# Causal attention inside a fused layer: fewer score maxima ahead of attention, folds between them, and maxima that go straight into the query operand

## The reference, cut to what matters

```python
def _attn(x, ln_w, ln_b, conv_w, attn_w, proj_w, n_head):
    h = _layernorm(x, ln_w, ln_b)
    ...  # causal convolution of 3 taps per channel
    q, k, v = jnp.split(h @ attn_w, 3, axis=-1)
    ...  # heads of D = 8, rotary embedding of q and k
    scores = jnp.einsum('bqhd,bkhd->bhqk', q, k) / jnp.sqrt(jnp.float32(D))
    scores = jnp.where(jnp.tril(jnp.ones((T, T), dtype=bool)), scores, jnp.float32(-1e+30))
    p = jax.nn.softmax(scores, axis=-1)
    y = jnp.einsum('bhqk,bkhd->bqhd', p, v).reshape(B, T, C)
    return y @ proj_w
```

## Time and profile before

| | |
|---|---|
| median of 3 runs | 385.88 us (384.13 to 386.39) |
| the profiled execution's own time | 381.65 us |
| its span, first to last instruction | 379.8 us |
| mean granted clock of TensorE | 0.953 |
| PE busy | 330.6 us (87%) |
| DVE busy | 244.9 us (64%) |
| ACT busy | 210.6 us (55%) |
| POOL busy | 99.3 us (26%) |

### The profile page before, as it was taken

The page is one execution under the profiler, slowest core; times in us unless marked ns, Lnnn a source line. Parts: engine busy times, 40 slices in busy tenths (PEclk is TensorE's granted clock), DMA queues, the critical chain, the costliest instruction groups (busy, mean ns, idle before and its releaser), DMA issues.

```text
span 379.8 us, 6492 instructions
## 1 busy us (share of the span) xinstructions
PE 330.6 (87%) x2287; PEld 224.6 (59%) x2287; DVE 244.9 (64%) x606; ACT 210.6 (55%) x619; POOL 99.3 (26%) x110
## 2 busy tenths in 40 slices
PE   2768999998999699999988995997889999999756
PEld 1236888664656345545534663565568788887645
DVE  5785865785898757733623651236977976886746
ACT  1377795273234345565675532233676766776984
POOL 3425572110600000000140121041267454445300
PEclk9997999999999669999999998799999999999986
DMA  7660000076963000009001002020001000000001
GB/s 227 193 196 2 2 0 2 10 251 173 301 181 94 10 0 2 2 16 325 6 28 50 0 14 63 2 76 1 24 27 29 0 3 0 3 0 3 0 2 55
DMA packets 21506, 22.53 MB, mean 59 GB/s; under 512 B 3517, under 2 KB 18269, under 8 KB 21469
## 3 DMA queue, kind: packets, MB, share of 16 engines
q1 hardware_dynamic: 19666, 20.02, 17.4%
q0 software_dynamic: 512, 1.05, 0.9%
q10 hardware_dynamic: 1296, 1.05, 0.9%
HBM read 14.32 MB, written 7.70 MB: 58 GB/s over the span
## 4 chain that ended last, share of the span: by engine, by line
PE 53%; DVE 24%; issue 6%; DMA 6%; ACT 5%; POOL 4%; POOLq 0%; ACTq 0%; DVEq 0%
PE PS L1198 45%; PE PS L1241 5%; DVE mB L774 5%; ACT big L1027 3%; DMA big<-scr_x 2%; DVE big L633 2%; POOL scr_x L525 2%; DVE XN L578 2%; DVE stats L567 1%; DMA X<-in_x 1%; DVE big L595 1%; DMA scr_x<-XN,pos 1%; DVE mraw L587 1%; DVE big L971 1%; PE PS L1208 1%
## 5 line engine op out<-in xcount | busy, mean ns | idle before, releaser
L1198 PE MATMUL PS<-big 128*128 128x128 f32 (+10 forms) x592 | 103.8, 324 | 12.5 <-DVE mB L774 4.9
L1198 PEld LDWEIGHTS PS<-big 128*128 128x128 f32 (+3 forms) x592 | 61.3, 155 | 50.3 <-issue 18.0
L1001 ACT ACTIVATE big<-PS 128x1280 f32<-128x1280 f32 (+2 forms) x44 | 41.0, 934 | 48.2 <-PE PS L1241 31.2
L482 POOL TENSOR_TENSOR big<-big,urec 128x1024 f32<-128x1024 f32 x24 | 45.6, 1900 | 65.8 <-DVE urec L626 44.6
L1027 ACT ACTIVATE big<-big 128x154 f32<-128x154 f32 x192 | 60.4, 319 | 4.1 <-DVE big L633 2.9
L1135 ACT ACTIVATE big<-PS 128x1024 f32<-128x1024 f32 (+3 forms) x64 | 42.6, 703 | 33.2 <-PE PS L1198 33.1
L774 DVE TENSOR_REDUCE mB<-PS 128x2 f32<-128x256 f32 (+5 forms) x86 | 51.0, 648 | 13.8 <-PE PS L1198 13.1
L1198 PE MATMUL PS<-cstb 128*128 128x128 bf16 x256 | 50.9, 228 | 0.0
L470 POOL TENSOR_TENSOR rstd<-ve,minus_half 128x4 f32<-128x4 f32 (+2 forms) x13 | 13.1, 1011 | 137.1 <-DVE ve L573 137.1
L1198 PE MATMUL PS<-kkC,XT 128*128 128x462 f32 (+1 forms) x96 | 36.2, 512 | 2.6 <-DVE big L633 2.6
L1027 ACT ACTIVATION_READ_ACCUMULATOR big<-big 128x1 f32 x192 | 36.3, 189 | 0.0
(11 more groups left out here) (174 smaller groups left out, 439.6 us busy)
## 6 DMA issues: line engine op xcount, KB each, us to landing
scr_qk<-big SPq DMA_DIRECT2D x12, 384.0 KB, 3.7
big<-scr_qk SPq DMA_DIRECT2D x16, 288.0 KB
big<-in_wv SPq DMA_DIRECT2D x1, 2048.0 KB, 9.5
scr_x<-zrow SPq DMA_DIRECT2D x2, 448.0 KB, 6.4
big<-scr_x SPq DMA_DIRECT2D x2, 448.0 KB, 4.3
scr_y<-big SPq DMA_DIRECT2D x2, 448.0 KB, 3.0
X<-in_x ACTq DMA_DIRECT2D x2, 256.0 KB, 3.7
big<-in_A_WoT ACTq DMA_DIRECT2D x1, 512.0 KB, 4.6
```

The source lines that it names most:

```text
L482: pool.tensor_tensor(pn[:, 0:GH * P].rearrange("p (h k) -> p h k", h=GH), Pt[u % 3][:, :, 0:KM], r.to_broadcast([P, GH, KM]), ALU.mult).th ...
L1001: return act.activation(dst, src, ACT.Copy, scale=scale)
L1198: return pe.matmul(o, lhsT, rhs, start=start, stop=stop)
```

## The change

- `PREC`: the vw/vr jobs of groups 2 and 3 (eight) come last; 42 jobs stand ahead of them (`F_VALUES`), and 46 ahead of those of group 3 (`F_BETWEEN`).
- Between the maxima of sequence 0 there is a fold after each odd m from 3, up to job 45. The other four follow after maxima 33 to 36, with their banks exchanged; job 47 needs the bank of the transposed maxima and waits for the first of their parts.
- `M_MERGE` is 38 (was 42) and `M_TURN` 33 (was 34): six maxima of sequence 1 ahead of attention, transposition after 32; `S_MAX` becomes 13 (was 11).
- Each of the three parts has its own semaphore step (`m_part`) and its own DMA from `nm3` to one row of `qs`; the scratch `scr_m` is gone.
- Attention's first pair waits for reduce 36, its second for 37 (both waited for 41).
- ScalarE lays out `vaug` from job 42 on, between four of the last copies.

```diff
+        F_VALUES = 42
+        F_BETWEEN = 46
...
-                if c >= 2 and c % 2 == 0:
+                if c in (2, 4):
                     for b in range(B):
                         yield "vw", (c // 2 - 1, b), 1
                         yield "vr", (c // 2 - 1, b), 1
+            for g in (2, 3):
+                for b in range(B):
+                    yield "vw", (g, b), 1
+                    yield "vr", (g, b), 1
...
         def fold_bank(n):
-            return n % 3 if n < F_LATE else 6 + n % 2
+            if n < F_LATE:
+                return n % 3
+            return 6 + n % 2 if n < F_BETWEEN else 7 - n % 2
...
-        M_TURN = 32 + 2
-        M_MERGE = 32+10
+        M_TURN = 32 + 1
+        M_MERGE = 32 + 6
         S_MAX = (64 - M_MERGE) // 2
...
             for b in range(B):
-                sp.wait_ge(m_split, b + 1)
-                sp.dma_start(scr_m[b].rearrange("a (n q) -> n a q", q=P), nm3[:, b]).then_inc(m_written[b], 16)
-                sp.wait_ge(m_written[b], 16)
                 sp.wait_ge(*((s1_mm, 2 * (64 - M_MERGE)) if b else (s_mm, 32)))
-                sp.dma_start(qs[b][SPLIT:SHIFT, :, :],
-                             scr_m[b].rearrange("a (h t) -> a h t", h=HB)).then_inc(m_ready[b], 16)
+                for a in range(3):
+                    sp.wait_ge(m_part[b], a + 1)
+                    sp.dma_start(qs[b][SPLIT + a:SPLIT + a + 1].rearrange("r h (t q) -> r (h t) q", q=P),
+                                 nm3[:, b, a]).then_inc(m_ready[b], 16)
...
-                own(dve.tensor_copy(nm3[:, b, 0], nmf[:, 0]))
-                own.wait()
+                dve.tensor_copy(nm3[:, b, 0], nmf[:, 0]).then_inc(m_part[b], 1)
+                dve.wait_ge(m_part[b], 1)
                 own(dve.tensor_tensor(nmf[:, 1], nmf[:, 0], nm3[:, b, 0], ALU.subtract))
                 own.wait()
-                own(dve.tensor_copy(nm3[:, b, 1], nmf[:, 1]))
-                own.wait()
-                dve.tensor_tensor(nm3[:, b, 2], nmf[:, 1], nm3[:, b, 1], ALU.subtract).then_inc(m_split, 1)
+                dve.tensor_copy(nm3[:, b, 1], nmf[:, 1]).then_inc(m_part[b], 1)
+                dve.wait_ge(m_part[b], 2)
+                dve.tensor_tensor(nm3[:, b, 2], nmf[:, 1], nm3[:, b, 1], ALU.subtract).then_inc(m_part[b], 1)
...
-            copy_C(F_LN, len(PREC))
-            def stack_values():
-                act.wait_ge(preC_act, N_PREC)
-                for b in range(B):
...
-            stack_values()
+            copy_C(F_LN, F_VALUES)
+            act.wait_ge(preC_act, sum(j[2] for j in PREC[:F_VALUES]))
+            for b in range(B):
...
+                copy_C(F_VALUES + 2 * b, F_VALUES + 2 * b + 1)
...
+                copy_C(F_VALUES + 2 * b + 1, F_VALUES + 2 * b + 2)
+            copy_C(F_VALUES + 2 * B, len(PREC))
...
+                    elif n == F_BETWEEN + 1:
+                        pe.wait_ge(m_part[0], 1)
...
                 if m == M_MERGE:
-                    pe.wait_ge(m_split, 1)
+                    pe.wait_ge(m_part[0], 1)
+                    pe.wait_ge(preC_act, N_PREC)
...
             for m in range(32):
                 scores_for_maximum(m)
-                if m >= 2 and m % 2 == 0 and late < len(PREC):
+                if m >= 3 and m % 2 == 1 and late < F_BETWEEN:
                     fold_C(late, late + 1)
                     late += 1
-            fold_C(late, len(PREC))
-            for m in range(32, M_MERGE):
+            for m in range(32, M_TURN):
                 scores_for_maximum(m)
-                if m == M_TURN - 1:
-                    pe.wait_ge(preC_act, N_PREC)
-                    turn_maxima(0)
+            pe.wait_ge(preC_act, sum(j[2] for j in PREC[:F_BETWEEN]))
+            turn_maxima(0)
+            for m in range(M_TURN, M_MERGE):
+                scores_for_maximum(m)
+                if late < len(PREC):
+                    fold_C(late, late + 1)
+                    late += 1
...
-                    pe.wait_ge(m_ready[b], 16)
+                    pe.wait_ge(m_ready[b], 16 * 3)
...
-                        pe.wait_ge(s_max, M_MERGE)
+                        pe.wait_ge(s_max, M_MERGE - 1 + pair)
```

More of the change, by code:

```diff
@@ L238, in program @@
         scr_y = [nc.dram_tensor(f"scr_y{b}", (SLOTS * P, D), F32, kind="Internal").ap() for b in range(B)]
-        scr_m = nc.dram_tensor("scr_m", (B, 3, HB * QT * P), BF16, kind="Internal").ap()
         F_UNIT = (3, 6, 9)
@@ L305, in program @@
         s1_mm, s1_max = sem("s1_mm"), sem("s1_max")
-        m_turned, m_split = sem("m_turned"), sem("m_split")
-        m_written = [sem(f"m_written{b}") for b in range(B)]
+        m_turned = sem("m_turned")
+        m_part = [sem(f"m_part{b}") for b in range(B)]
         m_ready = [sem(f"m_ready{b}") for b in range(B)]
@@ L1097, in _ @@
             ln_out("b", HT[:, :, 2:T + 2], *ln1, seqs=(1,))
-            copy_C(F_LN, len(PREC))
-            def stack_values():
-                act.wait_ge(preC_act, N_PREC)
-                for b in range(B):
-                    v = vaug[:, b].rearrange("p t h m -> p (t h) m")
-                    copy(v[:, :, 0:HDB], XN[:, QT * b:QT * b + QT, :].rearrange("p t (h d) -> p (t h) d", h=HB)).then_inc(v_ready, 1)
-                    copy(v[:, :, HDB:HDB + 1], ones[:, 0:QT * HB].unsqueeze(2)).then_inc(v_ready, 1)
-                    copy(v[:, :, HDB + 1:32], ones[:, 0:32 - HDB - 1].unsqueeze(1).to_broadcast([P, QT * HB, 32 - HDB - 1]),
-                         0.0).then_inc(v_ready, 1)
-            stack_values()
+            copy_C(F_LN, F_VALUES)
+            act.wait_ge(preC_act, sum(j[2] for j in PREC[:F_VALUES]))
+            for b in range(B):
+                v = vaug[:, b].rearrange("p t h m -> p (t h) m")
+                copy(v[:, :, 0:HDB], XN[:, QT * b:QT * b + QT, :].rearrange("p t (h d) -> p (t h) d", h=HB)).then_inc(v_ready, 1)
+                copy(v[:, :, HDB:HDB + 1], ones[:, 0:QT * HB].unsqueeze(2)).then_inc(v_ready, 1)
+                copy_C(F_VALUES + 2 * b, F_VALUES + 2 * b + 1)
+                copy(v[:, :, HDB + 1:32], ones[:, 0:32 - HDB - 1].unsqueeze(1).to_broadcast([P, QT * HB, 32 - HDB - 1]),
+                     0.0).then_inc(v_ready, 1)
+                copy_C(F_VALUES + 2 * b + 1, F_VALUES + 2 * b + 2)
+            copy_C(F_VALUES + 2 * B, len(PREC))
             act.wait_ge(scr_written[B - 1], 16 * 6)
@@ L1404, in turn_maxima @@
                 if b:
-                    pe.wait_ge(m_split, b)
+                    pe.wait_ge(m_part[0], 1)
                 pe.transpose(PS[0:HB * QT, 6, 0:P], mB[:, b].rearrange("p h t -> p (h t)"), ident).then_inc(m_turned, 1)
@@ L1466, in turn_outputs @@
                         pe.wait_ge(yg_ready, 4 * b + 4)
-                        pe.wait_ge(m_split, B)
+                        pe.wait_ge(m_part[B - 1], 1)
                         if b:
```

## The result

| | before | changed | ratio, 95% interval |
|---|---|---|---|
| median, first measurement | 385.71 us | 375.81 us (373.66 to 379.54) | 0.9741 [0.9691, 0.9791] |
| median, second measurement | 384.45 us | 377.28 us | 0.9783 [0.9733, 0.9833] |
| profiled execution, first measurement | 381.65 us, span 379.8 | 373.66 us, span 371.8 | |

The changed kernel is faster by 2.2 to 2.6%. Medians are of all executions of a kernel and ratios leave out its slow ones (over 1.5% above its fastest; one of four and one of six here), so the second ratio says -8.3 us where its medians say -7.2. The forecast was 378.9, in a range of 375.5 to 383.0; the first median lies 0.3 us above the range's lower end. The first question is where the 8.0 us between the two spans lie, since a trace is one execution.

A forecast was written before the change was run, and what follows sets the result against it. Three limits: a TensorE-VectorE loop, a hole, then TensorE alone, half of that at half clock. Terms -5.7 - 3.3 + 1.35 + 0.7 = -6.95 us took the median from 385.88 to 378.9, range 375.5 to 383.0.

The forecast's parts named there:

- end of the last reduce of sequence 0: Loop of sequence 0's maxima: moved folds spare three head pairs 0.35 us each, 1.05; taken as 1.0, bounds 0.3 to 1.1.
- from there to attention: Last reduce of sequence 0 to attention's start: 5.0 us instead of 9.74; with the earlier reduce, attention starts 5.7 sooner.
- attention, steps 0 to 4: Start of attention: the clock holds, so steps 0 to 3 take 9.76 instead of 13.02 us, -3.3.
- four tiles more: Attention steps 11 and 12: four more score tiles of sequence 1 cost +1.35 us (1.2 to 1.6).
- stand at step 16: Attention step 16: TensorE waits for sequence 1's maxima, transposed after step 13, not 11; +0.7 us (0 to 1.5).
- so VectorE's own sum binds: Loop of sequence 0's maxima: with folds moved, the two-engine loop falls under VectorE's 3.06 us a head pair.
- busy until T0+4.9: After sequence 0's last reduce (T0): transposition, five score tiles and four folds keep TensorE busy for 4.9 us.
- landed at T0+4.0, hidden by 0.9: Third part of sequence 0's maxima, issued 1.9 us after the last reduce (T0), lands at 4.0, 0.9 before attention needs it.
- B: Rival: the clock falls all the same in the hole before attention, the 3.3 us are gone, -3.65, 382.2 us; chance 0.13.
- C: Rival: direct DMAs are slow, 1.7 us a part, stands before attention and at step 16; +3.75, 389.6 us; chance 0.09.
- D: Rival: later stages' stands meet the clock otherwise and give back 3 us; -4, 381.9 us; chance 0.15.
- The row against the rule: Maxima transfers: a trace row's 197 GB/s was trusted over the port rule's some 27 GB/s, which would give -6.1 in all.

The follow-up runs named there:

- the even folds: Changed kernel with the 14 folds between sequence 0's maxima back behind even m (2 to 28); ratio 0.9853 to the kernel before.
- early-transposition kernel: Changed kernel with sequence 1's maxima transposed ahead of step 12's output matmuls, not behind; 374.83 against 383.17 us, again 375.03 against the changed kernel's 377.28.
- the fold ahead: Changed kernel with fold 46 moved ahead of the transposition of sequence 0's maxima, the other three behind maxima 34 to 36; 376.18 against 383.17 us.
- both moves: Changed kernel with fold 46 ahead of sequence 0's transposition and sequence 1's transposition ahead of step 12's output matmuls; 375.18 against 383.17 us.
- the load held: Changed kernel with the 2 MB expert weight load waiting on SyncE until step 16's first pair is scored; 377.83 against 384.45 us.

## Why the prediction came out as it did

By its own terms, with the changed kernel's first profile beside them:

| term | forecast | measured |
|---|---|---|
| end of the last reduce of sequence 0 | -1.05 | -2.12 (25.64 to 23.52 from the first reduce) |
| from there to attention | 5.0 for 9.74: -4.7 | 6.47: -3.27 |
| attention, steps 0 to 4 | -3.3 | -3.87 |
| four tiles more | +1.35 | +1.44 (19.26 - 1.16 - 16.66) |
| stand at step 16 | +0.7 | +1.16 |
| sum | -6.95 | -6.65 |

The mechanism was right. That the sum is this close is luck: the loop gave 1.1 us more than forecast and the way to attention 1.4 less.

**The loop.** The step "so VectorE's own sum binds" was right, its size was not. I took 3.06 for that sum because the timeline prints 16 reduces as one block of 12.22 us. A block without idle time in it doesn't say that the engine sets its pace: the even folds give 3.06 with both engines in the chain, VectorE was busy for 12.08 us of that block, and the new kernel gives 2.94. That is 8 x 0.12 = 1.0 us, nearly the whole error of this term (1.07).

**From there to attention.** Two things failed here, and either is enough. In the first profile it was the clock: "busy until T0+4.9" held for 1.00, and with some 3 us at half TensorE's own work fills 6.34 us. The third part wasn't last there. At full clock the share was sized rightly: in the early-transposition kernel TensorE works from 119.43 to 124.37, 4.94 us. There "landed at T0+4.0, hidden by 0.9" failed. Each issue takes 0.46 to 0.60 us and not 0.3 to 0.4, three in a row take 1.81, and in five of the profiles (the fold ahead, the early transposition, both moves, the load held, the changed kernel again) the slowest landing of sequence 0 took 3.3 to 3.8 us from its issue. In these five the clock was at 1.00 in this stretch, and attention starts 5.6 to 6.0 us behind the transposition, once that part is there. In all five, and in the even folds with 2.8, a 16 KB instruction packet started before the parts had all moved, and four packets of a part moved only at its end, as shown above. In the other five profiles with direct parts, and for sequence 1 in all eleven, no such packet ran beside them, and no landing took more than 2.3. What makes that packet come when it does, no experiment took apart.

**The clock.** In attention it held, as forecast, and by the first profile that is the largest term: 3.9 us. The forecast had it at 1.00 from 95 to 160. Around the transposition it was at 0.50 for 3.4 us in the changed kernel, in its forms with the scratch back and with ten maxima, and in the second profile of the early transposition, and for 6.8 us in the even folds. All five had a stand of 1.56 or 1.60 us ahead of the transposition, not the 1.1 of the forecast. So had the three profiles in which it held; behind 0.42 and 0.43 it held twice. Between two profiles of one kernel a fall of 3.4 us made 0.3 us (the changed kernel) and 0.6 (the early transposition), since where the clock holds the late third part costs something too; the fall of 6.8 cost 1.9.

A low clock in steps 0 to 4 costs 3 to 4.6: they took 12.2 to 13.8 us in seven kernels, and 9.15 or 9.16 in the others. The stand right ahead of step 0 (1.27 to 3.49 us in the seven) isn't the cause in all of them. In the kernel before, with direct DMAs alone and with six maxima alone the clock was already down when that stand began; it had fallen at the end of the one of 1.63 us or just behind it. With direct DMAs and six maxima it fell 0.2 us after that stand began. It fell behind that stand in three: ten maxima (1.64), the fold ahead (1.97) and both moves (1.52). Behind 1.43, 1.06, 1.03 and 0.71 us it held, and behind the 2.10 us of the earlier trace rows too, so length alone doesn't decide. What the change did is to leave no stand of over 1.1 us between the transposition and step 0.

**Four tiles and step 16.** Both were sized from the right rows. The stand is 0.5 longer than forecast, from the same three issues of 0.58. It is gone when the second transposition comes 1.6 us earlier (13.23 us behind step 8's first matmul, not 14.83).

**The rest of the distance.** The median is 3.1 us below the forecast, while the region alone gained 0.3 less than it. The changed kernel's runs lie from 373.66 to 382.34, and its two profiles differ by 6.5 us outside the region (371.8 - 68.17 and 377.9 - 67.81), with identical code. By the ratios the gain is 10.0 us (8.1 to 11.9) and 8.3 (6.4 to 10.3). The second holds the 6.95 and the 7.0 of its region, the first holds neither. Some 1.3 to 3.4 us of gain outside the region stay open: the kernel before has one profile, shorter than the timed runs beside it.

**The rivals.** B (the clock falls all the same) happened for 3 us, not for 13. In full it is what the profiles show without the folds' new places or with ten maxima; without the direct DMAs the loss comes at step 16 instead. C (slow direct DMAs) failed: mostly 2.2 us a landing, and a part moves in a quarter microsecond, not in 1.7 us. Its slower result was close, though, with another culprit, the trip through DRAM: six maxima without the direct parts are 8.8 us slower. D (later stages meet the clock otherwise): the stretch behind step 16 is 0.5 us longer than before in the first profile and 2.8 in the second, which has the new half-clock stretch at 195.9; the profiles of the even folds and of the load held have one there too. All three signs that the forecast had named against itself thus came true in some profile (a landing over 3 us, 0.50 between 120 and 140, 0.50 anew behind 185), and none was large enough to undo the gain.

**The row against the rule.** The row itself was misread. A window counts a packet where it starts: 0.68 of 16 engines for 0.25 us is 2.7 us of engine time, so the three 16 KB packets of the earlier trace rows took 0.9 us each, side by side. The wider window has no other bytes to speak of:

```profile
167.50:168.75 1.25, 1.25 (x16) 0.63 (x14) 0.00 (x0) 0.82 (x2) 0.00 (x0) 1.00 0.14 39
```

48 KB in 0.9 us is some 50 GB/s, not 197. For the direct parts there is now a row of their own: the quarter microsecond in the early-transposition kernel moves one whole part into one partition at 66 GB/s, 16.5 KB, in packets far shorter than the window. By 27 GB/s through one port (the Trainium skill, "SBUF — State Buffer", section "Door 1: The DMA port swizzle (why `[64,N]` ≈ `[32,N]`)") it would take 0.6, an estimate. So the sum was right not to go by the rule, for a smaller reason than it gave; what is slow in these small transfers is issue and landing, 0.58 and 2.2 us, not their bytes.

**Where the gain is from.** Against the kernel before, by the ratios: direct DMAs 0, six maxima +8.9 us, both 0, all but the direct DMAs 0 (+0.8, within its interval), all but the six maxima -2.5, all together -8 to -10. The folds' places alone were not run. Six maxima take 3.4 us out of the way to attention, if the parts come directly; four folds fill the gap that this leaves, and with them the clock holds in attention. The 3.0 us ahead of the transposition are 1.6 by the odd places (25.29 to 23.65) and 1.4 by three folds and one maximum fewer ahead of it (26.66 to 25.29). The forecast had these as separate terms of one sum and didn't say that most of it comes only when all three are there.

## What to carry to other kernels

When something long hides a transfer, shortening it alone can make the kernel slower: work out first what is late next, with its whole way (issue, write, read back), and change both. Look for stands of TensorE shortly ahead of a long stretch of it, where a lost clock costs most; moving filler work out of there to fill an earlier stand gained 0.4 us at most and lost 3 in the profiled executions. A block of back-to-back instructions in a timeline is the engine's own pace only if no other engine's work of the same period stands beside it in the chain and the stage table has the engine busy throughout. And a rate read in a window shorter than the packets is no rate.

## What the runs showed of the chip

- Three DMAs of 64 chunks of 256 bytes, one behind the other on SyncE, took 0.58 us each to issue (once 1.25, in the even folds) and mostly 2.1 to 2.3 us to land. For sequence 0 the slowest of three took 3.3 to 3.8 us in five profiles and 2.8 in the one of the even folds. In these six, and in no other case, a 16 KB packet of the queue "instruction" (0.9 to 1.3 us long) started before the parts had all moved, and four packets of a part moved only at its end.
- Attention's matmul that waits for the three rows read back from DRAM started 3.1 to 4.0 us after the issue of that read; the write before it had taken 2.07.
- With six maxima alone the clock was at 0.50 for 13 us, from 128 to 141, with TensorE busy for 9.51 of them; the long stand of 3.49 us lies inside. Behind the same stand of 1.56 us, with TensorE full from there on, it was at 0.50 for 3 us in one execution of the changed kernel and at 1.00 throughout in the other.
- The packets of one 16 KB part, 64 of 256 bytes from 64 partitions into one, all moved within a quarter microsecond (66 GB/s); three packets of 16 KB from DRAM, each into a partition of its own, took 0.9 us side by side.
